# Boundary diagonal on VectorE, the last FFN rows behind the first products, projections over three PSUM banks, and filling matmuls at other places

## The reference

```
O_lh, O_rh = polar_orthogonal(W_lh), polar_orthogonal(W_rh)   # 12 iterations of 1.5 X - 0.5 X X^T X
q = xn Wq^T ;  v = xn Wv^T
h_t = rms(h_{t-1} O_lh^T + q_t O_rh^T)      # a scan over the 512 rows of each sequence, h_0 = identity
attn = (h * v) Wc^T
ffn  = sqrt((xn cos(theta + theta_noise))^2 + (xn sin(phi + phi_noise))^2)
out  = x + attn + ffn
```

## Time and profile before

| what | us |
|---|---|
| median of the runs (3) | 161.42 |
| lowest and highest of them | 160.47, 161.51 |
| the profiled execution, its own time | 158.67 |
| its span, first to last instruction | 156.9 |
| PE busy | 119.8 (76%) |
| DVE busy | 94.3 (60%) |
| ACT busy | 83.9 (53%) |
| POOL busy | 56.2 (36%) |
| mean granted clock of TensorE | 0.937 |

### The profile page before, as it was taken

How to read it: one execution, slowest core, us unless ns; L and a number is a source line. 1 busy time by engine, 2 the same in 40 slices (tenths; PEclk the granted TensorE clock), 3 DMA queues, 4 the chain that set the end, 5 groups by cost and what they waited for, 6 DMA issues and landing times.

```text
span 156.9 us, 2766 instructions
## 1 busy us (share of the span) xinstructions
PE 119.8 (76%) x767; PEld 94.8 (60%) x767; DVE 94.3 (60%) x410; ACT 83.9 (53%) x307; POOL 56.2 (36%) x94
## 2 busy tenths in 40 slices
PE   6888888746977787889998866499986886877730
PEld 6666777735865675566665634477775775766510
DVE  3599999723442545555565563255578788888730
ACT  3146999975445666766867657133334344344300
POOL 7106778500010135655463563422223323323300
PEclk9999999999999999999999999755599999999975
DMA  4980000000000000000000000001010210110210
GB/s 120 267 298 3 0 6 0 0 0 4 0 0 2 0 0 0 4 0 0 0 2 2 2 0 0 4 0 53 14 67 0 73 67 2 67 67 4 102 34 10
DMA packets 3347, 5.00 MB, mean 32 GB/s; under 512 B 448, under 2 KB 1344, under 8 KB 3328
## 3 DMA queue, kind: packets, MB, share of 16 engines
q1 hardware_dynamic: 3024, 4.46, 8.4%
q0 software_dynamic: 160, 0.26, 0.5%
q10 hardware_dynamic: 144, 0.07, 0.1%
HBM read 2.69 MB, written 2.10 MB: 31 GB/s over the span
## 4 chain that ended last, share of the span: by engine, by line
PE 48%; DVE 26%; ACT 11%; issue 7%; POOL 3%; DVEq 1%; ACTq 0%; POOLq 0%
PE bank L896 8%; DVE W L664 8%; PE bank L904 7%; PE bank L853 6%; PE bank L768 4%; DVE WMID L647 3%; PE bank L863 3%; PE bank L812 3%; DVE SQM L652 3%; DVE bank L658 3%; PE bank L798 3%; PE bank L905 3%; PE bank L885 2%; DVE WTM L671 2%; PE bank L763 2%
## 5 line engine op out<-in xcount | busy, mean ns | idle before, releaser
L853 PE MATMUL bank<-IDENT,W 128*128 128x128 f32 x33 | 11.2, 340 | 14.7 <-DVE W L664 14.2
L293 POOL TENSOR_TENSOR FS<-FSQ 128x256 f32<-128x256 f32 x16 | 11.7, 733 | 27.5 <-ACT FSQ L429 27.5
L647 DVE SCALAR_TENSOR_TENSOR WMID<-UZ,RT,bank 128x129 f32<-128x129 f32 x33 | 11.6, 350 | 16.6 <-PE bank L904 14.4
L410 ACT ACTIVATE SQE<-W 128x129 f32<-128x129 f32 x35 | 10.9, 313 | 18.5 <-DVE W L664 18.5
L853 PEld LDWEIGHTS bank<-IDENT,W 128*128 128x128 f32 x33 | 4.7, 143 | 24.0 <-DVE W L664 24.0
L896 PE MATMUL bank<-WCT,PV 128*128 128x128 f32 x64 | 16.4, 343 | 2.7 <-POOL PV L324 2.7
L768 PE MATMUL bank<-ONES 128*128 128x128 bf16 x157 | 18.0, 237 | 0.0
L281 POOL TENSOR_SCALAR XN<-X,MV,RSTD 128x128 f32<-128x128 f32 x16 | 13.5, 846 | 11.7 <-DVE RSTD L569 11.7
L633 DVE COPY WT<-bank 128x128 f32<-128x128 f32 x33 | 9.6, 291 | 12.0 <-PE bank L853 12.0
L446 ACT ACTIVATE SQM<-WMID 128x129 f32<-128x129 f32 x16 | 5.0, 314 | 22.0 <-DVE WMID L647 22.0
L875 PE MATMUL bank<-CS,XNT 128*128 128x256 f32 x64 | 16.5, 380 | 0.0
(11 more groups left out here) (151 smaller groups left out, 272.3 us busy)
## 6 DMA issues: line engine op xcount, KB each, us to landing
X<-in_L_attn_x_dram SPq DMA_DIRECT2D x8, 256.0 KB, 5.9
out_dram<-OUT SPq DMA_DIRECT2D x7, 256.0 KB, 2.0
out_dram<-OUT SPq DMA_DIRECT2D x2, 128.0 KB, 1.7
WP<-in_L_attn_W_rh_dram ACTq DMA_DIRECT2D x1, 64.0 KB, 2.0
WP<-in_L_attn_W_lh_dram SPq DMA_DIRECT2D x1, 64.0 KB, 2.3
ANG<-in_L_ffn_theta_dram POOLq DMA_DIRECT2D x1, 64.0 KB, 3.7
WV<-in_L_attn_Wv_dram SPq DMA_DIRECT2D x1, 64.0 KB, 3.5
ANG<-in_L_ffn_phi_dram POOLq DMA_DIRECT2D x1, 64.0 KB, 3.5
```

The costliest lines, as they stand in the source:

```text
L647: dve.scalar_tensor_tensor(out=WMID[:, 0:E], in0=UZ[:, uz(j), 0:E], scalar=norm_of(m), in1=YB[:, 0:E], op0=ALU.mult, op1=ALU.add).then_inc ...
L853: pe.transpose(TB[:, 0:P], state(s)[:, 0:P], IDENT[:, :]).then_inc(t_done, 1)
```

## The change

Four edits:

1. DIAG of the two boundaries is made by DVE inside `end_prepared`, which now stands ahead of `mid` in the move before the boundary. `end_scaled` leaves POOL. The semaphore einv_ready counts both reciprocals.
2. On POOL, XF of part 15 runs behind PV of step 1, and SIZE2 behind PV of step 3.
3. The pairs use banks 6, 7 and 5 in turn (PAIR_BANK), and from pair 10 on banks 6 and 7. A pair waits only for the copy of the last pair in its bank. The lists say two pairs behind Y2 and one behind the transpose in moves 0 to 2, and one per move after that up to move 8, one move longer than before. The value halves go two per move in moves 10 to 15.
4. The filling matmuls are 2, 6 and 2 in place of 3, 3 and 4.

Besides, a few waits are made only where they are new: eps_ready in move 0 alone, the copies of pairs up to move 15, nt_copied for pair 0 alone.

```diff
-    PAIRS_A = {0: (1, 2, 3), 1: (5, 6), 2: (8, 9)}
-    PAIRS_B = {0: (4,), 1: (7,), 2: (10,), 3: (11,), 4: (12,), 5: (13,), 6: (14,), 7: (15,)}
+    PAIRS_A = {0: (1, 2), 1: (4, 5), 2: (7, 8)}
+    PAIRS_B = {0: (3,), 1: (6,), 2: (9,), 3: (10,), 4: (11,), 5: (12,), 6: (13,), 7: (14,), 8: (15,)}
+    PAIR_BANK = [6, 7, 5, 6, 7, 5, 6, 7, 5, 6, 7, 6, 7, 6, 7, 6]
     FFN_A = {m: m - 3 for m in range(3, 3 + STEPS // 2)}
-    V_A = {10: 2, 11: 4, 12: 6, 13: 8, 14: 10}
-    V_B = {8: 0, 9: 1, 10: 3, 11: 5, 12: 7, 13: 9, 14: 11, 15: 12, 16: 13, 17: 14, 18: 15}
+    V_A = {m: 2 * m - 19 for m in range(10, 16)}
+    V_B = {9: 0, **{m: 2 * m - 18 for m in range(10, 16)}, 16: 13, 17: 14, 18: 15}
...
-            def end_scaled(e):
-
-                pool.wait_ge(einv_ready, e + 1)
-                pool.tensor_scalar(DIAG[:, :], IDENT[:, :], EINV[:, 0:1], None, ALU.mult).then_inc(diag_ready, 1)
...
-            end_scaled(0)
             for f in range(STEPS // 2):
-                if f == FFN_A[GUESSES - 1]:
-                    end_scaled(1)
                 ffn_sum(f)
                 if f:
                     ffn_added(f - 1)
-            ffn_added(STEPS // 2 - 1)
-
-            pool.wait_ge(wt_ready, GUESSES + 1)
-            pool.tensor_tensor(SIZE2[:, :], edge(EDGE[(CHECK + 1) % 2]), edge(EDGE[(CHECK + 1) % 2]),
-                               ALU.mult).then_inc(S["size2_done"], 1)
...
                 pool.tensor_tensor(PV[:, j % 4, :], VT[:, tile(j)], wt[:, :], ALU.mult).then_inc(S["pv_done"], 1)
+                if j == 1:
+                    ffn_added(STEPS // 2 - 1)
+                if j == 3:
+                    pool.tensor_tensor(SIZE2[:, :], edge(EDGE[(CHECK + 1) % 2]), edge(EDGE[(CHECK + 1) % 2]),
+                                       ALU.mult).then_inc(S["size2_done"], 1)
...
-                         PJ[i % 2][:, 0:n * P].rearrange("p (a c) -> p a c", a=n)).then_inc(S["uz_copied"], 1)
+                         bank[PAIR_BANK[i]][:, 0:n * P].rearrange("p (a c) -> p a c", a=n)).then_inc(S["uz_copied"], 1)
...
                 dve.wait_ge(r_ready, s + 1)
-                dve.reciprocal(EINV[:, :], RT[:, j:j + 1])
+                dve.reciprocal(EINV[:, :], RT[:, j:j + 1]).then_inc(einv_ready, 1)
                 dve.reciprocal(EINV2[:, :], SSE[:, s % 2:s % 2 + 1]).then_inc(einv_ready, 1)
+                dve.wait_ge(einv_ready, 2 * e + 1)
+                dve.tensor_scalar(DIAG[:, :], IDENT[:, :], EINV[:, 0:1], None, ALU.mult).then_inc(diag_ready, 1)
...
-                dve.wait_ge(S["eps_ready"], 3)
-                dve.wait_ge(S["uz_copied"], min(m, len(PAIRS) - 1) + 1)
+                if m == 0:
+                    dve.wait_ge(S["eps_ready"], 3)
+                if m < len(PAIRS):
+                    dve.wait_ge(S["uz_copied"], m + 1)
...
                 j = MOVES[m][0]
+                if ends_pass(m + 1):
+                    end_prepared(m)
                 mid(m, j)
                 mid_norm(m)
                 second(m, j)
-                if ends_pass(m + 1):
-                    end_prepared(m)
                 end(m, j)
...
-                else:
-                    pe.wait_ge(S["uz_copied"], i - 1)
-                pe.wait_ge(S["nt_copied"], 1)
-                b = PJ[i % 2]
+                if PAIR_BANK[i] in PAIR_BANK[:i]:
+                    pe.wait_ge(S["uz_copied"], max(k for k in range(i) if PAIR_BANK[k] == PAIR_BANK[i]) + 1)
+                if i == 0:
+                    pe.wait_ge(S["nt_copied"], 1)
+                b = bank[PAIR_BANK[i]]
...
+                if f == 1:
+                    pe.wait_ge(S["uz_copied"], max(k for k in range(len(PAIRS)) if PAIR_BANK[k] == 5) + 1)
...
                     if j:
                         projected(j - 1)
-                        fill(3)
+                        fill(2)
...
                     pe.transpose(TM[:, 0:P], WMID[:, 0:P], IDENT[:, :]).then_inc(tm_done, 1)
-                    fill(3)
+                    fill(6)
...
                     projected(j)
-                    fill(4)
+                    fill(2)
```

More of the change, by code:

```diff
@@ L396, in root_of_state @@
                 e = bounds_before(s)
-                act.wait_ge(einv_ready, e + 1)
+                act.wait_ge(einv_ready, 2 * e + 2)
                 act.activation(REND[:, :], SSE[:, s % 2:s % 2 + 1], ACT.Sqrt,
@@ L635, in end_prepared @@
             def end_prepared(s):
-                j = step_of(s)
+                j, e = step_of(s), bounds_before(s)
                 dve.wait_ge(r_ready, s + 1)
-                dve.reciprocal(EINV[:, :], RT[:, j:j + 1])
+                dve.reciprocal(EINV[:, :], RT[:, j:j + 1]).then_inc(einv_ready, 1)
                 dve.reciprocal(EINV2[:, :], SSE[:, s % 2:s % 2 + 1]).then_inc(einv_ready, 1)
+                dve.wait_ge(einv_ready, 2 * e + 1)
+                dve.tensor_scalar(DIAG[:, :], IDENT[:, :], EINV[:, 0:1], None, ALU.mult).then_inc(diag_ready, 1)
             def mid(m, j):
-                dve.wait_ge(S["eps_ready"], 3)
-                dve.wait_ge(S["uz_copied"], min(m, len(PAIRS) - 1) + 1)
+                if m == 0:
+                    dve.wait_ge(S["eps_ready"], 3)
+                if m < len(PAIRS):
+                    dve.wait_ge(S["uz_copied"], m + 1)
                 dve.wait_ge(r_ready, m + 1)
```

## The result

The changed kernel takes 150.06 us (median of 4 runs, 148.48 to 150.33), beside 160.94 us for the kernel before (median of the three runs shown above and a fourth, 158.32 to 161.51). The ratio is 0.939 with a 95% interval of 0.924 to 0.955. The forecast was 151.2, with a range of 148.8 to 155.5. The profiled execution took 149.97 us, its span 147.9 us; 146.7 had been forecast for the span.

What follows compares the result with a forecast made beforehand. Taken as bound by latency, no engine full. 3.53 + 2.86 + 3.04 + 0.90 - 0.11 = 10.2 us saved, taken off the median of 161.42, gave 151.2 us, range 148.8 to 155.5.

Steps and rivals of the forecast that it cites:

- Edit 1, POOL's order: Head of the last pass: move 20 falls from 6.40 to 2.87 and the half clock behind it goes, 6.39 us saved.
- the clock falls all the same: Behind the second boundary: half clock stays, only the 2.3 us idle time is saved; as rival 155.1 us, chance 0.12.
- Edit 2, three banks: Moves 1 to 3: pairs no longer wait for ACT's late copies; 3.04 us saved in moves 1 and 2, 0.90 in 3.
- The extra copy: List of pairs one move longer: one more move with ACT's copy at 2.91 in place of 2.80, 0.11 us lost.
- Rival B: First three moves do not shorten, held by ACT's copies or a late PE: 2 to 3 us, 153.7, chance 0.07.
- Edit 3, DIAG on DVE: Boundaries: DIAG hides before WMID; first gain counted within the banks' saving, second none; bounds 0.1 gained to 0.7 lost.
- the rule on the shared port: DVE's DIAG and a POOL operation exclude each other; a DIAG slipping by 0.3 would cost move 18 some 0.7 us.
- Edit 4, filling: Ten filling matmuls per move at new places, before matmuls that wait for DVE anyway: 0, bounds plus or minus 0.8 us.
- The removed waits: Waits on eps_ready after move 0, copies after the last pair and nt_copied were met long before: 0.
- the further 1.0 of edit 2: Upper bound at move 3: if it ran like any other move it would save 1.9 us, not 0.90.
- Rival C: Last pass: fillers no longer hold the clock, 15 moves at half clock, 10.5 to 18 us more, middle 165.5, chance 0.04.
- D: DVE or POOL gives back 1 to 2 us (DIAG late, or XF(15) late for PV(2)): 152.7, chance 0.05.

Runs made afterwards that it cites:

- Experiment 2: Kernel before with 28 more filling matmuls ahead of the first projection, PE's wait for POOL left in place: median 156.26 us against 159.38.
- experiment 3: Changed kernel with POOL's old order (XF of part 15 and SIZE2 ahead of the first product): 151.54 us, ratio 0.957 to before.
- experiment 7: Changed kernel with 20 filling matmuls in PE's prelude wait for ACT's copy of O_l: 148.05 us, ratio 0.933.
- experiment 6: Kernel with the prelude filled (experiment 7), with the new lists of pairs but two banks in place of three: 150.24 us against 148.05.
- experiment 5: Kernel before with only DIAG moved to DVE, ahead of the first half of the move: one run, 157.28 us.
- experiment 9: Changed kernel with the two old DVE waits (eps_ready, copied pairs) back in every move: one run, 148.9 us.
- experiments 9 and 10: The second of the two: kernel with the prelude filled (experiment 7), with both old DVE waits put in twice: 148.62 us against 148.05.

## Why the prediction was right, and where it was not

**Edit 1, POOL's order.** Right in place and mechanism: the first projection runs behind the transpose, move 20 is 2.91, XF(15) and SIZE2 are hidden. On the two profiles it gave 3.49 + 2.99 = 6.48 against 6.39. Experiment 2 shows how it splits: 2.40 for the wait, the rest for the clock. The clock's share is one execution's. With the order undone in the changed kernel it was 0.6 in place of 4.0 (experiment 3), so what the edit is worth lay between 3.0 and 6.4 us in the traces; what decides it is not shown. My bound for "the clock falls all the same" (2.3) was the right size of the wait; taking 6.39 as if it belonged to every run was too sure.

**Edit 2, three banks.** 3.04 + 0.90 for moves 1 to 3 (3.94): at full clock (experiment 7) they take 2.78, 2.78 and 3.75, which is 4.01. The extra copy cost 0.06 where 0.11 was forecast. The forecast had the saving of edit 3 at the first boundary inside this, and so has the 4.01. Rival B fell: in experiment 7 no pair behind move 0 waits for a copy of ACT, and three pairs fit a move. My reading that the wait holds the transpose was right for move 0 of the kernel before (L863 ahead of L853); behind the transpose it holds Y1, which experiment 6 shows.

**Edit 3, DIAG on DVE.** Right: hidden, 0.37 gained at the first boundary, none at the second, where the shift matmul sets the end. POOL was idle when DIAG ran, at both boundaries of both profiles (the changed kernel and experiment 5), so the rule on the shared port was not put to the test.

**Edit 4, filling.** Forecast 0. The moves are 2.84 or 2.85 with either filling, so 0 is right for the path. Whether the new places are also worth something through the clock (half clock in move 20 with the old filling in two profiles of three, with the new one in none of six) is open.

**The removed waits, put at 0: this term was wrong.** One trace against one, they are worth 1.05 us between W of move 3 and the last W (experiment 9): in the last pass, where DVE has no idle time ahead of WMID, and in the moves 16, 26 and 34, which are 0.14 to 0.36 longer. I took "met long before" for "free". Whether it is the waiting or the place of the code that costs is open (experiments 9 and 10).

**What was missing from the sum**: the early half clock. It costs 2.23 up to the first W and 0.36 in move 1, and it is at a place that the change doesn't touch. With the removed waits taking about 1.05 off, it put the last W at 138.62 where 136.9 was forecast, and the profiled execution took 149.97 us where the sum gave 148.5. The median, though, came out 1.1 under the forecast: I had carried over the 2.75 us between the profiled execution of before (158.67) and its median (161.42), and after the change the two agree (149.97 and 150.06). So the moves were forecast well, but that the median came this close to 151.2 is in part luck: 1.5 too little on the trace and 2.7 too much on top of it. The later sets of runs of before have medians of 159.38, 159.18 and 159.55 and spread from 157.0 to 162.2, with mean clocks from 0.956 to 0.915: in the main, the longer the run, the lower the clock, though runs of 161.3 to 161.6 us with 0.928 or 0.929 need another cause as well. That the early fall is in most runs of before and was missing in its one profile fits this, and so do the seven of nine profiles of experiment 7; it isn't shown for before itself.

**The range.** Its low end does not follow from the terms: 151.2 less 0.8 for the fillers, 0.1 for edit 3 and the further 1.0 of edit 2 is 149.3, and without edit 2's 1.0 it is 150.3, where the forecast has 148.8 and 149.6.

Rival C (half clock through the last pass) and D (DVE or POOL late) did not show.

## What to carry to other kernels

Where PE waits for a short time in a stretch that is mostly latency, price the wait and the clock apart: fill the wait with useless matmuls while leaving it in place, and see what remains. Try it in every such gap, the ones in the prelude too, since a fall that one profile doesn't have may be in most runs. And take out waits that are met long before on an engine that has no slack: with them in, the same work took longer here. When a pair of buffers is emptied by an engine that serves the critical chain first, a third buffer can take that engine's order off the chain; here it was worth 0.95 us in each of three moves.

## What the runs showed that I had not expected

- With the same idle time of PE, 1.73 us, the clock fell in the profile after and not in the one before; around the same wait of PE on POOL, 2.15 to 2.31 us, lay 3.4, 6.8, 10.2 or 13.7 us at half clock. In the longest of these (99.6 to 113.25) PE was busy 11.92 of 13.65 us.
- With two waits more that are met long before, a move takes 0.03 us more where DVE is the last to be ready, and with four no more than with two.
- A table load of 1.28 us on ACT, moved behind two copies that don't need it, was worth 1.33 us at the first W (trace against trace).
